# Full-width products as two half-width products side by side in a four-layer graph network on one core

## The chip, the cores and the metric

The kernel runs on one core of a Trainium2 chip. The metric is the device time of one execution in microseconds (us); lower is better. A profiled execution of the kernel is shown beside the times. TensorE is the matrix engine, VectorE and ScalarE are the elementwise engines, GpSimd (POOL) and SyncE (SP) do little here but issue transfers.

## The reference

A dense adjacency matrix `adj` (8192 x 8192, fp32) is multiplied five times by an 8192 x 64 matrix, with a layer norm, a relu, a residual addition and small weight products around each:

```python
h = relu(layernorm(x)); y = h
for k in range(2):                       # layer 0, sweeps 1 and 2
    y = tanh(concat([adj @ y, y]) @ W0[k])
x = x + y
h = relu(layernorm(x)); x = x + adj @ (h @ W1) + bias            # layer 1, sweep 3
h = relu(layernorm(x)); x = x + adj @ (h * (u >= 0.1) / 0.9)     # layer 2, sweep 4
h = relu(layernorm(x))                                           # layer 3, sweep 5
x = x + concat([h, adj @ h / (rowsum(adj) + 1)]) @ W3.T
```

The kernel applies the weights behind the large product, (adj @ h) @ W.

## The kernel before, in words

**Blocks.** The adjacency matrix lies in device memory as 16 x 16 blocks of 512 x 512 numbers, 1 MB each. A block (i, j) takes part in five sweeps, once in each. 775 transfers on SP's queue bring blocks into a ring of 8 slots or into a few held ones, in the order of use; a slot is filled again when TensorE has used the block (and VectorE, if it takes row sums from it).

**Wide and narrow products.** `operand` holds, for each tile of 128 nodes, 128 columns: the 64 features of one sweep and the 64 of the next. Where a block can serve two consecutive sweeps at once, `two_products` (line 632) multiplies it by all 128 columns: four fp32 matmuls with a stationary 128 x 128 operand and a moving 128 x 512 tile. The result has one sweep's features on partitions 0 to 63 and the other's on 64 to 127. Where it serves one sweep, `one_product` (line 604) multiplies it by 64 columns: in each of four steps the first 256 nodes go to partitions 0 to 63 and the other 256 to partitions 64 to 127, with the same stationary 128 x 64 operand. The accumulators are two banks each for wide rows (`double_acc`), narrow rows (`single_acc`), groups taken out of turn (`spare`) and row products (`natural`).

```python
# two_products
acc[:, :], operand[:, b.j * TPB + t, :], stream[:, t, :]
# one_product, h = 0, 1
acc[half_of(h), 0:HALF], operand[:, b.j * TPB + t, half_of(b.row.half)], stream[:, t, nodes_of(h)]
```

**The order of the work.** `make_plan` writes one list, `PLAN`, that all engines follow. Sweeps 1 and 3 run downwards, 2, 4 and 5 upwards, so that the blocks on one side of the diagonal serve two sweeps. A row of 512 nodes has narrow blocks ("single"), wide blocks ("double") and groups out of turn ("late", narrow, and "early", wide). After a row's sum VectorE writes it to `stack` (`take_first`, `take_doubles`); TensorE's `post` multiplies the stacked 128 features by the layer's weights into `natural`; ScalarE or VectorE finishes the row, whose values are an operand of the next sweep. A post is put one block into the next row.

**Own features.** Sweeps 1, 2 and 5 also need the row's own operand, transposed, on the other half of `stack`. ScalarE's `pair_own` copies it, paired, to `own_by_pair` (in sweep 5 four scalings by the degree), TensorE's `turn` transposes it in two full-width transposes into a spare bank, and ScalarE copies it to `stack`. In sweep 1 and 2 the copies are issued a row ahead; in sweep 5 two.

**Posts.** In sweeps 1, 2, 3 and 5 `post` makes eight fp32 products, 64 nodes each as the stationary operand and the 64 weight columns moving, onto alternating halves of the partitions. In sweep 4, whose layer has no weights, it makes two full-width transposes instead, and VectorE writes `stack` in two pieces for them. `degrees` adds the row sums once, by three full-width products.

In the trace each fp32 matmul leaves two MATMUL and two LDWEIGHTS records, a transpose one of each.

Of the kernel before, what the change touches and what calls it, by code (L numbers as in the profile page):

```python
# [36 lines left out]
F = 64  # L37
P = 128
# [387 lines left out]
def gnn_kernel(nc, adj, x, w_both, w_own, bias, u, identity, ones, out):  # L426
# [5 lines left out]
    with ctx:  # L432
# [6 lines left out]
        def sem(name):  # L439
            return ctx.enter_context(nc.semaphore(name))  # L440
# [13 lines left out]
        stack = sb("stack", [P, 2, BLOCK])  # L454
        own_by_pair = sb("own_by_pair", [P, 2, 2, 2 * F])
        deg_part = sb("deg_part", [P, 2 * BLOCK])
# [54 lines left out]
        own_ready = sem("own_ready")  # L511
        own_paired = sem("own_paired")
        tanh_ready = sem("tanh_ready")
# [70 lines left out]
        @block.gpsimd  # L584
        def _(pool):
            pool.memset(w_stack[:, 2, :], 0.0).then_inc(weights_cleared, 1)
            pool.memset(deg_quarter[:, 1:], 0.0).then_inc(deg_cleared, 1)
            for row in ROWS:
                if row.sweep == 3:
                    pool.wait_ge(norm_ready, row.r - 1 - NB)  # L590
                    pool.dma_start(u_in[:, row.r % 2], u[:, tiles(row.i), :]).then_inc(u_loaded[row.r % 2], 16)

        @block.tensor
        def _(pe):
# [37 lines left out]
            def two_products(b, acc):  # L632
                stream = tiles_of(b)
                for t in range(TPB):
                    last = nc.tensor.matmul(  # L635
                        acc[:, :], operand[:, b.j * TPB + t, :], stream[:, t, :],
                        start=b.first and t == 0, stop=b.last and t == TPB - 1)
                return last
# [14 lines left out]
            def turn(row):  # L653

                wait_new(consts_loaded, 16 * CONSTS)
                wait_new(own_paired, rows_with_own(row.r))
                acc = next_spare()
                for k in range(2):
                    last = nc.tensor.transpose(acc[:, k * P:(k + 1) * P], own_by_pair[:, row.r % 2, k, :], ident[:, :])  # L659
                last.then_inc(turned, 1)  # L660

            def post(row):
# [14 lines left out]
                acc = natural[row.r % 2]  # L677
                if row.sweep == 4:
                    to = acc[:, 0:TPB * F].rearrange("p (h k f) -> p k h f", h=2, k=2)
                    for k in range(2):  # L680
                        last = nc.tensor.transpose(to[:, k], stack[:, row.r % 2, k * P:(k + 1) * P],  # L681
                                                   ident[:, :].rearrange("p (h f) -> p h f", h=2))
                else:
                    for t in range(TPB):
                        for c in range(2):
                            nodes = slice(t * P + c * F, t * P + (c + 1) * F)
                            last = nc.tensor.matmul(acc[half_of(c), t * F:(t + 1) * F], stack[:, row.r % 2, nodes],  # L687
                                                    w_stack[:, row.sweep - 1, :], start=True, stop=True)
                last.then_inc(posted, 1)
# [26 lines left out]
        def _(act):  # L716
# [7 lines left out]

            def pair_own(row):

                wait_operand(act.wait_ge, row.sweep, row.i)
                slot = row.r % 2
                if row.sweep == SWEEPS:
                    act.wait_ge(deg_taken, 1)  # L730
                    for t in range(TPB):
                        at = (t % 2) * 2 * F + (t // 2) * F
                        last = nc.scalar.activation(
                            own_by_pair[:, slot].rearrange("p k f -> p (k f)")[:, at:at + F],
                            operand[:, row.i * TPB + t, half_of(row.half)], ACT.Copy, scale=deg_plus[:, row.i, t:t + 1])
                else:
                    own = operand[:, tiles(row.i), half_of(row.half)].rearrange("p (h k) f -> p k h f", k=2)
                    last = nc.scalar.copy(own_by_pair[:, slot].rearrange("p k (h f) -> p k h f", h=2), own)
                last.then_inc(own_paired, 1)

# [7 lines left out]
            act.dma_start(w_stack[upper, 1, :], w_own[lower, 0, :]).then_inc(consts_loaded, 16)  # L748
            act.dma_start(w_stack[lower, 1, :], w_both[lower, 1, :]).then_inc(consts_loaded, 16)
            act.dma_start(w_stack[lower, 4, :], w_own[lower, 1, :]).then_inc(consts_loaded, 16)  # L750
            for to, of in ((bias_sb, bias), (ident, identity)):
                act.dma_start(to[:], of[:]).then_inc(consts_loaded, 16)

            pair_own(ROWS[0])
            for g in range(2, NGROUPS):
                deviation(GROUP, g % 2)
            for what, row in PLAN:
# [8 lines left out]
                elif what == "turn":  # L766
                    if row.r == (SWEEPS - 1) * NB:
                        pair_own(row)
                        pair_own(ROWS[row.r + 1])
                    act.wait_ge(turned, rows_with_own(row.r))  # L770
# [4 lines left out]
                    if row.sweep == SWEEPS and row.i >= 2:  # L775
                        pair_own(ROWS[row.r + 2])
                    elif row.sweep < SWEEPS and row.i != (NB - 1 if row.sweep == 1 else 0):
                        pair_own(ROWS[row.r + 1])
                elif what == "post":
                    if row.sweep <= 2:  # L780
                        act.wait_ge(posted, row.r + 1)
                        got = natural[slot][:, 0:TPB * F].rearrange("p (t f) -> p t f", t=TPB)
                        to = operand[:, tiles(row.i), F:2 * F] if row.sweep == 1 else tanh_out[:, slot]
                        nc.scalar.activation(to, got, ACT.Tanh).then_inc(tanh_ready, 1)  # L784
                        if row.r == NB - 1:
                            pair_own(ROWS[NB])
                    if row.sweep in (2, 3, 4):
# [8 lines left out]
        def _(dve):  # L796
# [83 lines left out]
            def take_first(row):  # L880
# [12 lines left out]
                if not row.single:  # L893
                    if row.sweep == 4:
                        for h in range(2):
                            last = nc.vector.tensor_copy(stack[half_of(h), row.r % 2, 0:HALF], partial[part, row.i, nodes_of(h)])
                    else:
                        last = nc.vector.tensor_copy(stack[part, row.r % 2, :], partial[part, row.i, :])
                else:
# [9 lines left out]
            def take_doubles(row):  # L909
# [6 lines left out]
                else:  # L916
# [5 lines left out]
                    before = partial[part, row.i, :]  # L922
                if row.sweep == 4:
                    for h in range(2):
                        last = nc.vector.tensor_tensor(stack[half_of(h), row.r % 2, 0:HALF], got[part, nodes_of(h)],  # L925
                                                       before[:, nodes_of(h)], ALU.add)
                else:
                    last = nc.vector.tensor_tensor(stack[part, row.r % 2, :], got[part, :], before, ALU.add)  # L928
                last.then_inc(sums_ready, 1)
# [142 lines left out]
```

## Time and profile before

| | before |
|---|---|
| median of 3 runs | 2338.46 us (2338.21 to 2338.47) |
| the profiled execution | 2338.78 us |
| its span | 2337.0 us |
| TensorE busy | 2291.0 us, 98% |
| VectorE busy | 1066.8 us, 46% |
| ScalarE busy | 161.4 us, 7% |
| transfers | 820.78 MB, mean 351 GB/s |

The span is the time between the first and the last record of the profiled execution; what lies between it and the execution's own time (1.8 us) is outside the records. Busy time counts overlapping records once. In the views PE is TensorE's matmul and PEld its weight load, DVE is VectorE, ACT ScalarE; L635 is line 635 of the kernel. A timeline row merges instructions that follow each other and are of one kind; its duration runs to the end of the last record, which overlaps the start of the next row, so that paces are taken from the starts of consecutive rows.

### The profile page before, as it was taken

Reading aid. Unit: us, or ns where it says so; the run is one execution under the profiler, and the core shown is the slowest. Engines: PE = TensorE matmul, PEld = TensorE weight load, DVE = VectorE, ACT = ScalarE, POOL = GpSimd, SP = SyncE. Lnnn points to the kernel's source line nnn. Section 1 sums busy time; section 2 is a strip of 40 time slices with the busy share of each in tenths; the row PEclk is TensorE's granted clock in tenths of the full one; section 3 lists DMA queues with packets and bytes.
Section 4 is the critical chain, followed back from the end, with each engine's and each line's share of the span. In section 5 each row is a group of like instructions: output and inputs, shape, how many; then the busy total and the mean of one; then the engine's idle time right before and its main releaser. Section 6 shows DMA issues by size and latency. Waiting matters only on the chain.

```text
span 2337.0 us, 24750 instructions
## 1 busy us (share of the span) xinstructions
PE 2291.0 (98%) x10118; PEld 1131.9 (48%) x10118; DVE 1066.8 (46%) x2066; ACT 161.4 (7%) x366; POOL 9.5 (0%) x22
## 2 busy tenths in 40 slices
PE   6999999999999999999999999999999999999998
PEld 3454545545454444444444444444455455444465
DVE  7111102114554288887799878887423111101023
ACT  1000000000002210100100000000000000000022
POOL 0000000000000000000000000000000000000000
PEclk9999999999999999999999999999999999999999
DMA  9999999999998878788868888886899999999998
GB/s 388 421 421 421 387 381 378 397 347 377 390 382 293 288 287 303 291 305 300 350 252 356 299 306 310 315 331 256 302 376 389 388 371 389 378 381 376 396 405 363
DMA packets 117904, 820.78 MB, mean 351 GB/s; under 512 B 13856, under 2 KB 18080, under 8 KB 18592
## 3 DMA queue, kind: packets, MB, share of 16 engines
q1 hardware_dynamic: 113904, 814.79, 89.8%
q10 hardware_dynamic: 3120, 2.31, 0.3%
q0 software_dynamic: 768, 2.10, 0.3%
q8 instruction: 80, 1.31, 0.2%
q14 instruction: 32, 0.26, 0.0%
HBM read 817.05 MB, written 2.10 MB: 351 GB/s over the span
## 4 chain that ended last, share of the span: by engine, by line
PE 92%; DMA 5%; DVE 2%; SPq 0%; issue 0%; ACT 0%; DVEq 0%
PE double_acc L635 58%; PE spare L635 12%; PE single_acc L611 11%; PE spare L611 9%; DMA ring<-in_adj 4%; PE natural L687 1%; DMA resid<-in_x 1%; PE spare L659 1%; DVE centred L822 0%; DVE stats L810 0%; DVE partial L878 0%; SPq L574 0%; SPq L581 0%; DVE moments L813 0%; PE natural L681 0%
## 5 line engine op out<-in xcount | busy, mean ns | idle before, releaser
L635 PE MATMUL double_acc<-ring,operand 128*128 128x512 f32 x3136 | 1367.6, 594 | 4.1 <-DVE operand L993 2.6
L635 PEld LDWEIGHTS double_acc<-ring,operand 128*128 128x128 f32 x3136 | 588.9, 190 | 728.2 <-issue 716.5
L611 PE MATMUL single_acc<-ring,operand 128*64 128x256 f32 x2624 | 302.0, 384 | 28.4 <-DVE operand L836 21.8
L635 PE MATMUL spare<-ring,operand 128*128 128x512 f32 x680 | 298.9, 595 | 2.2 <-DMA ring<-in_adj 2.2
L878 DVE TENSOR_TENSOR partial<-spare,partial 64x256 f32<-64x256 f32 (+1 forms) x226 | 105.1, 465 | 421.7 <-PE spare L635 285.2
L859 DVE TENSOR_TENSOR deg_part<-deg_part,ring 128x1024 f32<-128x1024 f32 x213 | 260.9, 1225 | 7.3
L858 DVE TENSOR_TENSOR deg_part<-deg_part,ring 128x1024 f32<-128x1024 f32 x213 | 260.8, 1224 | 6.7
L611 PEld LDWEIGHTS single_acc<-ring,operand 128*64 128x64 f32 x2624 | 183.6, 138 | 150.2 <-DVE operand L836 27.4
L611 PE MATMUL spare<-ring,operand 128*64 128x256 f32 x1840 | 204.7, 380 | 2.1 <-DVE partial L878 2.1
L635 PEld LDWEIGHTS spare<-ring,operand 128*128 128x128 f32 x680 | 126.7, 190 | 157.6 <-issue 154.6
L611 PEld LDWEIGHTS spare<-ring,operand 128*64 128x64 f32 x1840 | 130.8, 137 | 79.5 <-issue 17.5
L925 DVE TENSOR_TENSOR stack<-double_acc,partial 64x256 f32<-64x256 f32 x30 | 12.8, 427 | 319.5 <-PE double_acc L635 319.3
L765 ACT COPY partial<-double_acc 64x512 f32<-64x512 f32 x45 | 26.0, 579 | 1051.7 <-PE double_acc L635 1051.7
L928 DVE TENSOR_TENSOR stack<-double_acc,stack 64x512 f32<-64x512 f32 x26 | 17.7, 682 | 128.6 <-PE double_acc L635 128.5
L822 DVE TENSOR_SCALAR centred<-resid,moments,rsd 128x64 f32<-128x64 f32 x256 | 62.9, 310 | 2.3
L904 DVE TENSOR_TENSOR stack<-single_acc,partial 64x256 f32<-64x256 f32 x80 | 33.6, 420 | 51.4 <-issue 34.9
L784 ACT ACTIVATE operand<-natural 128x256 f32<-128x256 f32 x16 | 6.1, 383 | 643.3 <-PE natural L687 643.3
L687 PEld LDWEIGHTS natural<-w_stack,stack 128*64 128x64 f32 x1024 | 37.9, 138 | 22.8 <-issue 13.2
L928 DVE TENSOR_TENSOR stack<-double_acc,partial 64x512 f32<-64x512 f32 x19 | 13.1, 690 | 73.3 <-PE double_acc L635 73.2
L810 DVE BATCH_NORM_STATS2 stats<-resid 128x6 f32<-128x64 f32 x256 | 38.7, 214 | 12.1 <-DMA resid<-in_x 10.3
L877 DVE COPY partial<-spare 128x512 f32<-128x512 f32 (+1 forms) x19 | 11.5, 607 | 70.3 <-PE spare L635 68.9
L723 ACT ACTIVATE sd<-moments,eps 128x4 f32<-128x4 f32 x64 | 18.9, 297 | 356.0 <-DVE moments L813 356.0
(60 smaller groups left out, 603.5 us busy)
## 6 DMA issues: line engine op xcount, KB each, us to landing
ring<-in_adj SPq DMA_DIRECT2D x756, 1024.0 KB, 7.2
held<-in_adj SPq DMA_DIRECT2D x17, 1024.0 KB, 9.0
resid<-in_x SPq DMA_DIRECT2D x16, 128.0 KB, 16.0
kept<-in_adj SPq DMA_DIRECT2D x2, 1024.0 KB, 11.6
for_layer<-in_u POOLq DMA_DIRECT2D x16, 128.0 KB, 2.4
out_rows<-for_layer ACTq DMA_DIRECT2D x16, 128.0 KB, 7.2
ident<-in_identity ACTq DMA_DIRECT2D x1, 64.0 KB, 10.8
w_stack<-in_w_both ACTq DMA_DIRECT2D x1, 48.0 KB, 8.1
```

The lines of the kernel that those rows point to most:

```text
L611: last = nc.tensor.matmul(acc[half_of(h), 0:HALF], operand[:, b.j * TPB + t, half_of(b.row.half)], stream[:, t, nodes_of(h)], start=b.firs ...
L635: last = nc.tensor.matmul(acc[:, :], operand[:, b.j * TPB + t, :], stream[:, t, :], start=b.first and t == 0, stop=b.last and t == TPB - 1)
L659: last = nc.tensor.transpose(acc[:, k * P:(k + 1) * P], own_by_pair[:, row.r % 2, k, :], ident[:, :])
L687: last = nc.tensor.matmul(acc[half_of(c), t * F:(t + 1) * F], stack[:, row.r % 2, nodes], w_stack[:, row.sweep - 1, :], start=True, stop=True)
L765: nc.scalar.copy(partial[other, row.i, :], double_acc[slot][other, :]).then_inc(partial_saved, 1)
L810: last = nc.vector.bn_stats(stats[:, slot, t, :], values[:, t, :])
L822: last = nc.vector.tensor_scalar(centred[:, t, :], values[:, t, :], moments[:, slot, t, 0:1], rsd[:, t:t + 1], ALU.subtract, ALU.mult)
L858: link(nc.vector.tensor_tensor(acc, acc, data[:, 0:2 * BLOCK], ALU.add))
L859: nc.vector.tensor_tensor(acc, acc, data[:, 2 * BLOCK:], ALU.add).then_inc(deg_added, 1)
L878: return nc.vector.tensor_tensor(to, got, to, ALU.add)
L904: last = nc.vector.tensor_tensor(to, got[half_of(h), 0:HALF], partial[part, row.i, nodes_of(h)], ALU.add)
L928: last = nc.vector.tensor_tensor(stack[part, row.r % 2, :], got[part, :], before, ALU.add)
```

## The change

The wide product becomes two half-width products, one for each sweep's 64 features, each with the whole moving tile of 512 nodes and its own half of the partitions. The turn takes the own operand straight from `operand` (in sweep 5 from a scaled copy) as stationary operand and multiplies it by the identity, on the half of the partitions where it is wanted; the paired copies of sweeps 1 and 2 are gone. The row products of sweep 4 go through the same eight products as the others, with an identity as weights, and VectorE writes `stack` in one piece. The degree sum is as it was.

```diff
-        own_by_pair = sb("own_by_pair", [P, 2, 2, 2 * F])
+        scaled = sb("scaled", [P, 2, TPB, F])
...
-            pool.memset(w_stack[:, 2, :], 0.0).then_inc(weights_cleared, 1)
+            pool.memset(w_stack[:, 2:4, :], 0.0).then_inc(weights_cleared, 1)
...
                 for t in range(TPB):
-                    last = nc.tensor.matmul(
-                        acc[:, :], operand[:, b.j * TPB + t, :], stream[:, t, :],
-                        start=b.first and t == 0, stop=b.last and t == TPB - 1)
+                    for half in range(2):
+                        last = nc.tensor.matmul(
+                            acc[half_of(half), :], operand[:, b.j * TPB + t, half_of(half)], stream[:, t, :],
+                            start=b.first and t == 0, stop=b.last and t == TPB - 1)
...
-                wait_new(own_paired, rows_with_own(row.r))
+                if row.sweep == SWEEPS:
+                    wait_new(own_scaled, row.r + 1 - (SWEEPS - 1) * NB)
+                else:
+                    wait_operand(wait_new, row.sweep, row.i)
                 acc = next_spare()
                 for k in range(2):
-                    last = nc.tensor.transpose(acc[:, k * P:(k + 1) * P], own_by_pair[:, row.r % 2, k, :], ident[:, :])
+                    for h in range(2):
+                        t = 2 * h + k
+                        own = scaled[:, row.r % 2, t, :] if row.sweep == SWEEPS else operand[:, row.i * TPB + t, half_of(row.half)]
+                        last = nc.tensor.matmul(acc[half_of(h), k * P:(k + 1) * P], own, ident[:, :], start=True, stop=True)
...
-                if row.sweep == 4:
-                    to = acc[:, 0:TPB * F].rearrange("p (h k f) -> p k h f", h=2, k=2)
-                    for k in range(2):
-                        last = nc.tensor.transpose(to[:, k], stack[:, row.r % 2, k * P:(k + 1) * P],
-                                                   ident[:, :].rearrange("p (h f) -> p h f", h=2))
-                else:
-                    for t in range(TPB):
-                        for c in range(2):
-                            nodes = slice(t * P + c * F, t * P + (c + 1) * F)
-                            last = nc.tensor.matmul(acc[half_of(c), t * F:(t + 1) * F], stack[:, row.r % 2, nodes],
-                                                    w_stack[:, row.sweep - 1, :], start=True, stop=True)
+                for t in range(TPB):
+                    for c in range(2):
+                        nodes = slice(t * P + c * F, t * P + (c + 1) * F)
+                        last = nc.tensor.matmul(acc[half_of(c), t * F:(t + 1) * F], stack[:, row.r % 2, nodes],
+                                                w_stack[:, row.sweep - 1, :], start=True, stop=True)
...
-                else:
-                    own = operand[:, tiles(row.i), half_of(row.half)].rearrange("p (h k) f -> p k h f", k=2)
-                    last = nc.scalar.copy(own_by_pair[:, slot].rearrange("p k (h f) -> p k h f", h=2), own)
-                last.then_inc(own_paired, 1)
...
-            act.dma_start(w_stack[lower, 1, :], w_both[lower, 1, :]).then_inc(consts_loaded, 16)
+            act.dma_start(w_stack[lower, 1:4:2, :], w_both[lower, 1:4:2, :]).then_inc(consts_loaded, 16)
...
-                if row.sweep == 4:
-                    for h in range(2):
-                        last = nc.vector.tensor_tensor(stack[half_of(h), row.r % 2, 0:HALF], got[part, nodes_of(h)],
-                                                       before[:, nodes_of(h)], ALU.add)
-                else:
-                    last = nc.vector.tensor_tensor(stack[part, row.r % 2, :], got[part, :], before, ALU.add)
+                last = nc.vector.tensor_tensor(stack[part, row.r % 2, :], got[part, :], before, ALU.add)
```

## Rows read from the trace of the kernel before

**Rows 1.** The page: span, TensorE's busy time, its granted clock in 40 slices

```profile
span 2337.0 us, 24750 instructions
PE 2291.0 (98%) x10118; PEld 1131.9 (48%) x10118; DVE 1066.8 (46%) x2066; ACT 161.4 (7%) x366; POOL 9.5 (0%) x22
...
PEclk9999999999999999999999999999999999999999
```

**Rows 2.** Table of stretches: length, busy time by engine, clock, DMA share, GB/s

```profile
157.00:716.00 559.00, 558.92 (x2666) 281.88 (x2666) 155.40 (x203) 19.33 (x51) 0.00 (x0) 1.00 0.97 383
716.00:755.00 39.00, 35.65 (x240) 19.91 (x240) 18.33 (x66) 14.37 (x27) 0.00 (x0) 1.00 0.85 301
755.00:1162.00 407.00, 406.77 (x1135) 182.36 (x1136) 292.44 (x409) 56.90 (x95) 0.67 (x1) 1.00 0.82 303
...
1192.00:1638.00 446.00, 445.90 (x1435) 203.86 (x1433) 369.51 (x535) 11.43 (x27) 6.44 (x12) 1.00 0.82 307
...
1661.00:2225.00 564.00, 563.41 (x2359) 279.62 (x2360) 99.56 (x345) 11.86 (x27) 0.00 (x0) 1.00 0.96 379
2225.00:2337.00 112.00, 102.71 (x1088) 68.01 (x1084) 33.38 (x121) 28.80 (x98) 0.00 (x0) 0.99 0.94 386
```

**Rows 3.** Chain that ended last, in order of time: start, us, what

```profile
142.62 14.24 DMA ring<-in_adj
...
2306.51 18.49 DMA ring<-in_adj
```

**Rows 4.** Groups of instructions, TensorE, shapes apart: the wide products

```profile
L635 PE MATMUL double_acc<-ring,operand 128*128 128x512 f32 x3136 | 1367.6, 594 | 4.1 <-DVE operand L993 2.6 <-DVE operand L988 1.3
...
L635 PE MATMUL spare<-ring,operand 128*128 128x512 f32 x680 | 298.9, 595 | 2.2 <-DMA ring<-in_adj 2.2
...
L635 PE MATMUL double_acc<-held,operand 128*128 128x512 f32 x24 | 10.6, 596 | 0.0
```

**Rows 5.** Timeline of TensorE in sweep 4: start, us, engine, line, tiles, count

```profile
1790.03 12.31 PE L611 MATMUL spare<-ring,operand 128*64 128x256 f32 x112
1802.27 3.70 PE L635 MATMUL double_acc<-ring,operand 128*128 128x512 f32 x8
1805.81 0.38 PE L681 MATMUL natural<-ident,stack 128*128 128x128 f32 x2
1806.03 24.20 PE L635 MATMUL double_acc<-ring,operand 128*128 128x512 f32 x56
1830.15 10.58 PE L611 MATMUL spare<-ring,operand 128*64 128x256 f32 x96
1840.66 3.70 PE L635 MATMUL double_acc<-ring,operand 128*128 128x512 f32 x8
```

**Rows 6.** Timeline of TensorE: a row product among narrow products

```profile
1162.65 1.95 PE L611 MATMUL single_acc<-held,operand 128*64 128x256 f32 x16
1164.43 0.63 PE L687 MATMUL natural<-w_stack,stack 128*64 128x64 f32 x16
1164.90 3.63 PE L611 MATMUL spare<-ring,operand 128*64 128x256 f32 x32
```

**Rows 7.** Timeline of TensorE: the degree sum

```profile
1713.58 1.46 PE L698 MATMUL spare<-deg_quarter,fold_sb 128*128 128x256 f32 x6
1714.87 1.45 PE L635 MATMUL double_acc<-ring,operand 128*128 128x512 f32 x3
```

**Rows 8.** Timeline of TensorE: a turn of sweep 2

```profile
1015.26 0.38 PE L659 MATMUL spare<-ident,own_by_pair 128*128 128x128 f32 x2
1015.48 1.45 PE L635 MATMUL double_acc<-ring,operand 128*128 128x512 f32 x3
```

**Rows 9.** Table of one stretch, line 659 (turns), then line 681 (posts, sweep 4)

```profile
157.00:2225.00 2068.00, 11.90 (x58) 6.94 (x58) 1.00 0.90 345
...
157.00:2225.00 2068.00, 5.84 (x30) 4.06 (x30) 1.00 0.90 345
```

**Rows 10.** Waits of TensorE: us in total, times, longest

```profile
PE single_acc L611 <- DMA ring<-in_adj: 6.2, 10, 0.9
```

More of the change, by code:

```diff
@@ L511, in gnn_kernel @@
         own_ready = sem("own_ready")
-        own_paired = sem("own_paired")
+        own_scaled = sem("own_scaled")
         tanh_ready = sem("tanh_ready")
@@ L723, in deviation, with scale_own @@
                 nc.scalar.activation(sd[:, slot, 0:n], moments[:, slot, 0:n, 1], ACT.Sqrt, bias=eps[:, 0:1]).then_inc(sd_ready, 1)
-            def pair_own(row):
+            def scale_own(row):
                 wait_operand(act.wait_ge, row.sweep, row.i)
[L728 to L735, printed above, removed]
-                else:
-                    own = operand[:, tiles(row.i), half_of(row.half)].rearrange("p (h k) f -> p k h f", k=2)
-                    last = nc.scalar.copy(own_by_pair[:, slot].rearrange("p k (h f) -> p k h f", h=2), own)
-                last.then_inc(own_paired, 1)
+                act.wait_ge(deg_taken, 1)
+                for t in range(TPB):
+                    last = nc.scalar.activation(scaled[:, row.r % 2, t], operand[:, row.i * TPB + t, half_of(row.half)],
+                                                ACT.Copy, scale=deg_plus[:, row.i, t:t + 1])
+                last.then_inc(own_scaled, 1)
             act.wait_ge(eps_set, 1)
@@ L752, in _ @@
                 act.dma_start(to[:], of[:]).then_inc(consts_loaded, 16)
-            pair_own(ROWS[0])
             for g in range(2, NGROUPS):
@@ L767, in _ @@
                     if row.r == (SWEEPS - 1) * NB:
-                        pair_own(row)
-                        pair_own(ROWS[row.r + 1])
+                        scale_own(row)
+                        scale_own(ROWS[row.r + 1])
                     act.wait_ge(turned, rows_with_own(row.r))
@@ L775, in _ @@
                     if row.sweep == SWEEPS and row.i >= 2:
-                        pair_own(ROWS[row.r + 2])
-                    elif row.sweep < SWEEPS and row.i != (NB - 1 if row.sweep == 1 else 0):
-                        pair_own(ROWS[row.r + 1])
+                        scale_own(ROWS[row.r + 2])
                 elif what == "post":
@@ L784, in _ @@
                         nc.scalar.activation(to, got, ACT.Tanh).then_inc(tanh_ready, 1)
-                        if row.r == NB - 1:
-                            pair_own(ROWS[NB])
                     if row.sweep in (2, 3, 4):
@@ L893, in take_first @@
                 if not row.single:
-                    if row.sweep == 4:
-                        for h in range(2):
-                            last = nc.vector.tensor_copy(stack[half_of(h), row.r % 2, 0:HALF], partial[part, row.i, nodes_of(h)])
-                    else:
-                        last = nc.vector.tensor_copy(stack[part, row.r % 2, :], partial[part, row.i, :])
+                    last = nc.vector.tensor_copy(stack[part, row.r % 2, :], partial[part, row.i, :])
                 else:
@@ L922, in take_doubles @@
                     before = partial[part, row.i, :]
-                if row.sweep == 4:
-                    for h in range(2):
-                        last = nc.vector.tensor_tensor(stack[half_of(h), row.r % 2, 0:HALF], got[part, nodes_of(h)],
-                                                       before[:, nodes_of(h)], ALU.add)
-                else:
-                    last = nc.vector.tensor_tensor(stack[part, row.r % 2, :], got[part, :], before, ALU.add)
+                last = nc.vector.tensor_tensor(stack[part, row.r % 2, :], got[part, :], before, ALU.add)
                 last.then_inc(sums_ready, 1)
```

## The prediction

> **What bounds the kernel now.** I read the page first: TensorE is busy for 98% of the span at the full granted clock, the higher of its two levels [rows 1]. No other engine comes near. The table of stretches says where its pace really counts: from 157 us to 2225 us it is never out of work for long, while the last 112 us show gaps [rows 2]. The chain of waits says what bounds the two ends: until 157 us and from about 2225 us it runs through transfers of adjacency blocks [rows 3], and there TensorE only follows. In between stand three short stretches at the turn from one sweep to the next (716 to 755, 1162 to 1192, 1638 to 1661 us), where VectorE's normalisation chain is waited for; the first of them is in [rows 2]. So a shorter stream on TensorE is worth its full length between 157 and 2225 us, about half in the three turns, and nothing at the ends.
>
> The stream is of two kinds. Each fp32 product leaves two records, so a wide block (two sweeps, 128 columns) is 8 records of 512 elements, and a narrow one (one sweep, 64 columns) 16 records of 256 that run two by two. The groups give 3136 and 680 and 24 wide records, thus 480 wide blocks [rows 4]. The mean duration of a record is no pace, since records overlap; the pace comes from starts in the timeline [rows 5]. Two wide runs: 1806.03 to 1830.15 is 24.12 us for 56 records, 1802.27 to 1805.81 is 3.54 us for 8. A step of 0.429 us makes 24.02 and 3.43, which leaves about 0.10 us over in each: in the first because a narrow run follows and starts late, in the second because it comes from a narrow run and its first weight load lies open (it goes over into a full-width transpose without loss). Two narrow runs: 12.24 us for 56 pairs, 10.51 us for 48. The difference, 1.73 us over 8 pairs, is 0.216 us a pair, and each run has 0.15 us over. What a run has too much is a late start of the next (0.09 either way) and an open load at its own start (0.10 wide, 0.05 narrow). A round trip costs 0.10 + 0.10 + 0.15, unrounded **0.347 us**, and these leftovers are what the change removes. That the width does it, not the length of the stream or the accumulator, is in [rows 6]: a narrow block at 1162.65 (after a wide one) is followed by a row product, narrow too but with 64 elements and another bank, after 8 x 0.216 + 0.05 = 1.78 us: the open load alone. The next narrow run starts 0.47 us later.
>
> The Trainium skill (TensorEngine Tiling (Array Packing), Key Properties) says that changing the tiling mode drains the array. The trace agrees, at about 0.09 us each way; the open load comes on top.
>
> **The change, part by part.**
>
> (a) *Wide products as two halves.* 3840 records become 7680 in 3840 pairs. The trace has no pair with 512 elements. Below lies a step of 0.427 us (the 512 elements at the pace of rows, without overhead); above, the nearest row is a pair whose halves do not overlap at all, 2 x 0.429. The value comes from a direct comparison: the degree sum has six undivided records of 256 elements in 1713.58 to 1714.87, 0.215 us each [rows 7], and a pair of half-width ones of the same length has 0.216. Doubling the length doubles the step and adds nothing to it (0.215 against 0.429). I take 0.429 for the pair: cost 0. Its cover: the loads of the next pair run under the present one, as they do now in a narrow pair, which is half as long. If that cover goes, rival 2 has the price.
>
> A second rule speaks against it. The Trainium skill (TensorE: Matmul & The Clock Gate, Part 3) gives a packed group the time of one matmul plus about 4 ns for each further tile; by that rule the sum would lose 15 us and come to 2336.5, where the rows give 2321.5 (an estimate from that page). The narrow pairs here show 1 ns or less.
>
> (b) *Changes of width removed.* TensorE's timeline has 198 of them, 163 between 157 and 2225 us; [rows 5] shows five. Outside the three turns these are 75 round trips (31 to 716 us, 12 to 1162, 18 to 1638, 14 to 2225): 75 x 0.347 = 26.0 us. In 13 of them the first wide work is an own-feature turn, whose load is 0.05 shorter: less 0.6. **Gain 25.4 us.** One round trip is new: the degree sum keeps full width and stood among wide blocks. **Cost 0.35 us.**
>
> (c) *Turns.* Two transposes of one record each take 0.22 us, 1015.26 to 1015.48 [rows 8]. They become four fp32 products, 8 records in 4 pairs, each with 128 elements streaming. A record of that length steps 0.11 us in the same row, so 0.44 us. Ends: 0.06 a pair, the pace of the 64-element pairs of a post (0.47 us over 8 pairs [rows 6]), or 0.22 a pair, that of a pair of 256. 0.11 is the row of the same length. Between 157 and 2225 us there are 58 records [rows 9], 29 turns, 25 outside the three stretches: 25 x 0.22 = **cost 5.5 us**, ends 0 and 16.
>
> (d) *Row products of sweep 4.* Two transposes in 0.22 us (1805.81 to 1806.03 [rows 5]) become the 16 records that every other sweep uses, 0.47 us [rows 6]. Of 15 before 2225 us (30 records [rows 9]) thirteen lie outside the three stretches: 13 x 0.25 = **cost 3.3 us**, ends 0 (the records hidden in the run around them) and 6 (twice the price).
>
> (e) *Other queues.* ScalarE loses the 32 pairing copies of sweeps 1 and 2; the turn then waits for the operand itself, which is ready earlier. The four scalings for sweep 5 stay. VectorE's sums of sweep 4 are one instruction in place of two. Both have slack outside the three stretches; cost 0 there. At the first turn of sweeps a copy less stands ahead of the tanh, some tenths at most. SP and POOL issue what they did; one weight transfer carries one block more, at the very start. The cleared weights reach over one block more.
>
> (f) *The three stretches.* Eight round trips (2.8 us) against 4 turns (0.9) and 2 posts (0.5): 1.4 us shorter, half of it lost to waiting for VectorE: **gain 0.7 us**. At the ends, gain and cost both vanish behind transfers: sweep 5 has 16 of the 48 turns there, 0.22 us more each, but the last stretch follows the transfers, one 1 MB block at a time [rows 3].
>
> Sum: 25.4 - 0.35 - 5.5 - 3.3 + 0.7 = **17.0 us**. The profiled execution took 2338.78 us with a span of 2337.0; it becomes 2321.8. The median of the runs stands 0.3 us under the profiled one: **2321.5 us**. What becomes late next is nothing new; the transfers' share between 157 and 716 us (0.97) and after 1661 (0.96) [rows 2] leaves 3% or more, and 8 us of 559 and 2 us of 564 are asked for.
>
> **Rivals.**
>
> 1. *The gain is held up by transfers or VectorE.* If the stretches with 0.97 and 0.96 [rows 2] are transfer-bound, only 755 to 1638 us gains: 30 round trips, 10.4 us, less 12 turns, 2.6: 7.8 us, **2331**. For it: those shares. Against: TensorE's narrow blocks wait for ring transfers 6.2 us in all, at the ends [rows 10], and VectorE is busy 370 of the 446 us from 1192 on, where it is busiest [rows 2]. Chance 0.10.
>
> 2. *Slower: the weight loads of the two halves are not covered.* Place: each pair in a wide block. The price of an open narrow load is the 0.05 us of [rows 5]. Of the 3840 wide steps 97 come before 157 us, so about 3740 count: +187 us, less the 17 gained, **2508**. It decides from 17.0 / 3740 = 4.5 ns a pair on, a tenth of a load. Against: narrow pairs already load both halves under a stream half as long. Chance 0.07. The Trainium skill (same page, Part 3) says that loads overlap running matmuls only if their row groups differ, and the halves share all rows; the narrow pairs contradict it.
>
> 3. *A few ns more for each pair.* The two halves read the same moving tile a few ns apart; 4 ns by 3740 is 15 us, **2336.5**, no change. Against: 0.216 against 0.215. The rule of the skill weighed in (a) is this case. Chance 0.07.
>
> 4. *The change does not do what it says:* the 0.09 us stay, because they belong to another stream or bank, and only the open loads go. 75 x 0.15 = 11 less 9 is 2 to 3 us, **2336**. [Rows 6] speaks against it. Chance 0.02.
>
> **How the numbers follow.** The forecast has 0.74. About 0.2% (4.7 us) is what a measurement of this kernel can tell from no change. The forecast and rival 1 are faster beyond it, rivals 3 and 4 within it, rival 2 slower; a little is moved from faster to the others, for a pair step off by 3 to 5 ns: 0.82, 0.10, 0.08. The range: below, turns and sweep-4 posts near their low ends give 6 us more, 2315.5; above, turns at their high end cost 10.5 more, 2332, and rival 1 stands at 2331: 2331.5. It leaves out rivals 2 to 4, 0.16.
>
> **What would show it.** In the profile after: a wide block of 16 records in 3.43 us, pair step 0.429; no leftover between wide and narrow runs; 8 records in 0.44 us for a turn and 16 in 0.47 for a sweep-4 post; waits for VectorE at the turns of sweeps longer by about a microsecond; a last stretch of the same length. Wrong it would be if the pair step were 0.433 or more, or if TensorE waited for transfers between 157 and 2225 us.

## The result, and the profile after

| | before | after |
|---|---|---|
| median | 2338.47 us (2338.21 to 2338.72, 4 runs) | 2322.78 us (2322.38 to 2323.25, 4 runs) |
| ratio | | 0.9933, 95% interval 0.9921 to 0.9944 |
| the profiled execution, its span | 2338.78, 2337.0 us | 2323.25, 2321.4 us |

The kernel is 15.7 us (0.67%) faster. Forecast were 2321.5 us and a gain of 17.0, in a range of 2315.5 to 2331.5. A second measurement of the same kernel gave 2322.20 us against 2338.62 before, ratio 0.9931 (0.9917 to 0.9944).

The page of the changed kernel: span and busy time, the costliest groups of the wide products, and VectorE's sums (out<-in xcount | busy, mean ns of one | idle time before).

```profile
span 2321.4 us, 33389 instructions
PE 2273.9 (98%) x14470; PEld 976.4 (42%) x14470; DVE 1064.2 (46%) x2050; ACT 150.3 (6%) x334; POOL 9.6 (0%) x22
...
PEclk9999999999999999999999999999999999999999
...
L636 PE MATMUL double_acc<-ring,operand 128*64 128x512 f32 x6272 | 1362.9, 592 | 4.5 <-DVE operand L973 3.1
...
L636 PE MATMUL spare<-ring,operand 128*64 128x512 f32 x1360 | 297.3, 592 | 2.3 <-DMA ring<-in_adj 2.2
...
L908 DVE TENSOR_TENSOR stack<-double_acc,partial 64x512 f32<-64x512 f32 x34 | 23.5, 692 | 390.9 <-PE double_acc L636 390.8
```

TensorE has 4352 records more than before and is busy 17 us less. The wide groups of [rows 4] have twice the records and nearly the same busy time (1367.6 before, 1362.9 now), as a pair takes the time that one record took. The granted clock is full as in [rows 1], so no part of the difference is a clock.

The part of sweep 4 that answers to [rows 5], in TensorE's timeline after (start, duration, instructions):

```profile
1775.31 12.26 PE L611 MATMUL spare<-ring,operand 128*64 128x256 f32 x112
1787.39 3.60 PE L636 MATMUL double_acc<-ring,operand 128*64 128x512 f32 x16
1790.83 0.63 PE L688 MATMUL natural<-w_stack,stack 128*64 128x64 f32 x16
1791.29 24.20 PE L636 MATMUL double_acc<-ring,operand 128*64 128x512 f32 x112
1815.33 10.53 PE L611 MATMUL spare<-ring,operand 128*64 128x256 f32 x96
1825.69 3.60 PE L636 MATMUL double_acc<-ring,operand 128*64 128x512 f32 x16
```

From start to start, before and after: 56 narrow pairs 12.24 and 12.08 us; a wide block 3.54 and 3.44; the row product 0.22 and 0.46; seven wide blocks 24.12 and 24.04; 48 narrow pairs 10.51 and 10.36. The leftovers of 0.15, 0.10 and 0.08 are gone: 24.04 / 56 is 0.4293 us for a pair, 12.08 / 56 is 0.2157. Over all steady wide steps of the two traces the mean is 0.4292 us both before and after. The row product costs 0.24 more, so that of a round trip of 0.35 some 0.1 is left where sweep 4 has both.

The answer to [rows 8], a turn of sweep 2: 0.43 us from start to start, where it was 0.22.

```profile
1007.38 0.61 PE L666 MATMUL spare<-ident,operand 128*64 128x128 f32 x8
1007.81 3.60 PE L636 MATMUL double_acc<-ring,operand 128*64 128x512 f32 x16
```

The answer to [rows 6], in the timeline after, the row product among narrow ones:

```profile
1154.29 1.90 PE L611 MATMUL single_acc<-held,operand 128*64 128x256 f32 x16
1156.01 0.63 PE L688 MATMUL natural<-w_stack,stack 128*64 128x64 f32 x16
1156.48 3.63 PE L611 MATMUL spare<-ring,operand 128*64 128x256 f32 x32
```

The narrow block that followed a wide one now starts without its open load: 1.72 us to the row product, where it was 1.78. The row product itself keeps its 0.47. And the answer to the first of [rows 3], in the chain that ended last (start, us, what):

```profile
142.28 15.07 DMA ring<-in_adj
```

The transfer that the chain follows up to 157 us ends 0.49 us later than it did before (157.35 against 156.86), so nothing is gained until there.

The gain can be read at any place that both timelines have, by the start of the same block. At the borders of the stretches in [rows 2], each time at the block that starts nearest to the border, it grows like this, beside what the prediction's prices give for each stretch:

```
stretch of before   gain measured   by the prediction's prices
157 to 716 us          7.03         31 x 0.347 - 0.65 - 13 x 0.22        = 7.2
716 to 755             0.12
755 to 1162            1.71         12 x 0.347 - 12 x 0.22               = 1.5
1162 to 1192           0.18
1192 to 1638           5.63         18 x 0.347                           = 6.2
1638 to 1661           0.19
1661 to 2225           1.17         14 x 0.347 - 13 x 0.25 - 0.35        = 1.3
sum                   16.03         (three short stretches together 0.7) = 17.0
```

In the second measurement of the changed kernel the seven numbers are the same to 0.01 us. What differs between these two executions lies outside: the first 157 us and the last 110.

### The profile page after: what moved, and what is told of

Read it like the earlier page. It is cut to its first block, busy times and chain, and to the rows that moved or that the text cites. A ratio compares the mean times of both kernels' runs of the same rounds, so it can differ in the third digit from the quotient of the medians.

```text
span 2321.4 us, 33389 instructions
## 1 busy us (share of the span) xinstructions
PE 2273.9 (98%) x14470; PEld 976.4 (42%) x14470; DVE 1064.2 (46%) x2050; ACT 150.3 (6%) x334; POOL 9.6 (0%) x22
## 4 chain that ended last, share of the span: by engine, by line
PE 91%; DMA 6%; DVE 2%; issue 0%; SPq 0%; ACT 0%; DVEq 0%
PE double_acc L636 58%; PE spare L636 12%; PE single_acc L611 10%; PE spare L611 9%; DMA ring<-in_adj 5%; PE natural L688 1%; DMA resid<-in_x 1%; PE spare L666 1%; DVE centred L811 0%; DVE partial L867 0%; DVE stats L799 0%; DVE moments L802 0%; SPq L574 0%; SPq L581 0%; ACT sd L724 0%
## 5 line engine op out<-in xcount | busy, mean ns | idle before, releaser
L636 PE MATMUL double_acc<-ring,operand 128*64 128x512 f32 x6272 | 1362.9, 592 | 4.5 <-DVE operand L973 3.1
L636 PEld LDWEIGHTS double_acc<-ring,operand 128*64 128x64 f32 x6272 | 445.4, 137 | 860.1 <-issue 846.4
L636 PE MATMUL spare<-ring,operand 128*64 128x512 f32 x1360 | 297.3, 592 | 2.3 <-DMA ring<-in_adj 2.2
L908 DVE TENSOR_TENSOR stack<-double_acc,partial 64x512 f32<-64x512 f32 x34 | 23.5, 692 | 390.9 <-PE double_acc L636 390.8
L636 PEld LDWEIGHTS spare<-ring,operand 128*64 128x64 f32 x1360 | 97.0, 137 | 182.8 <-issue 177.3
L611 PEld LDWEIGHTS spare<-ring,operand 128*64 128x64 f32 x1840 | 132.7, 137 | 75.4 <-issue 13.5
L688 PEld LDWEIGHTS natural<-w_stack,stack 128*64 128x64 f32 x1280 | 49.5, 138 | 29.6 <-issue 16.5
L688 PE MATMUL natural<-w_stack,stack 128*64 128x64 f32 x1280 | 50.1, 222 | 4.0 <-DVE stack L908 1.9
L866 DVE COPY partial<-spare 128x512 f32<-128x512 f32 (+1 forms) x19 | 11.5, 607 | 70.6 <-PE spare L636 69.2
```

What stands on the lines that cost most here:

```text
L611: last = nc.tensor.matmul(acc[half_of(h), 0:HALF], operand[:, b.j * TPB + t, half_of(b.row.half)], stream[:, t, nodes_of(h)], start=b.firs ...
L636: last = nc.tensor.matmul(acc[half_of(half), :], operand[:, b.j * TPB + t, half_of(half)], stream[:, t, :], start=b.first and t == 0, stop ...
```

## The experiments

**One part alone: the wide products.** The kernel before with this edit only:

```diff
                 for t in range(TPB):
-                    last = nc.tensor.matmul(
-                        acc[:, :], operand[:, b.j * TPB + t, :], stream[:, t, :],
+                    for half in range(2):
+                        last = nc.tensor.matmul(
+                            acc[half_of(half), :], operand[:, b.j * TPB + t, half_of(half)], stream[:, t, :],
```

> The kernel before with the wide products as two halves, and nothing else: turns and the row products of sweep 4 stay full-width transposes. Theory (every change of width costs a drain of 0.09 us and an open load): between 157 and 2225 us 163 changes of width become 90, all around the 29 turns, 15 posts of sweep 4 and the degree sum, at 0.093 + 0.056 + 0.094 + 0.05 = 0.293 us a round trip. Against the changed kernel that is 44 x 0.293 = 12.9 us more, less 29 x 0.22 + 15 x 0.25 = 10.1 for the cheaper transposes: +2.5 to 2.8, about 2325.4 us. Rival A (the gain comes from ScalarE and VectorE, which have less to do): no gain here, 2338. Rival B (the identity products in half width are a loss that should have been left out): this kernel beats the changed one, 2312 to 2315.

Measured: 2325.18 us, ratio 0.9941 (0.9926 to 0.9956). That is 2.4 us above the changed kernel, as the theory has it. The two were not measured side by side; the kernel before took 2339.15 us beside this one and 2338.47 beside the other. The traces need no such comparison: between the block that starts at 157 us and the one at 2225 us this kernel gains 13.2 us on the kernel before, where the changed kernel gains 16.0. The timeline of this kernel shows both kinds of transposes standing alone in full width, first a turn, then a row product of sweep 4:

```profile
1009.09 0.44 PE L660 MATMUL spare<-ident,own_by_pair 128*128 128x128 f32 x2
1009.45 3.65 PE L636 MATMUL double_acc<-ring,operand 128*64 128x512 f32 x16
...
1792.80 0.44 PE L682 MATMUL natural<-ident,stack 128*128 128x128 f32 x2
1793.17 24.25 PE L636 MATMUL double_acc<-ring,operand 128*64 128x512 f32 x112
```

A transposing turn or row product now takes 0.36 to 0.37 us (0.22, its load open for 0.05, the late start behind it 0.09), and with the late start ahead and the open load after, the round trip has eaten what the transposes save. Rival A is out: ScalarE and VectorE work as they did before, and all but 2 to 3 us of the gain is there. Rival B is out too: the identity products pay, by a little.

**The other part alone.** The changed kernel with `two_products` as it was before, so that only turns and row products are in half width.

> The changed kernel with the wide products undivided again: only turns and the row products of sweep 4 are half-width. Theory: 211 changes of width between 157 and 2225 us against 163 before, 24 round trips more at 0.347 us = 8.3, 29 turns x 0.22 = 6.4 and 15 posts x 0.25 = 3.8: 18.5 us more than before, less about 1.5 hidden between the sweeps: slower, about 2356 us. Rival A (less work for ScalarE and VectorE brings the gain): at or under 2338. Sum check: the two parts alone give about -13 and +17, together -15.7, so the parts must not add up.

Measured: 2357.64 us, ratio 1.0080 (1.0065 to 1.0095), slower by some 18.5 us where about 17 was expected. The turn and the wide block behind it in this kernel:

```profile
1025.33 0.66 PE L665 MATMUL spare<-ident,operand 128*64 128x128 f32 x8
1025.92 3.70 PE L635 MATMUL double_acc<-ring,operand 128*128 128x512 f32 x8
1029.55 0.69 PE L687 MATMUL natural<-w_stack,stack 128*64 128x64 f32 x16
```

The turn is 0.59 us (0.44 and 0.15 of an open load and a late start), the wide block 3.63 (3.43 and 0.20). The two parts are worth about 14.0 and -18.5 us alone (both against 2339.15 us, the kernel before measured beside them) and 15.7 together: the identity products in half width pay only where the products around them are in half width too.

**More round trips, and nothing else changed.** In the changed kernel every second wide block of the rows of sweeps 2 and 3 is undivided again:

```diff
+                if b.row.sweep in (2, 3) and b.j % 2:
+                    for t in range(TPB):
+                        last = nc.tensor.matmul(
+                            acc[:, :], operand[:, b.j * TPB + t, :], stream[:, t, :],
+                            start=b.first and t == 0, stop=b.last and t == TPB - 1)
+                    return last
                 for t in range(TPB):
                     for half in range(2):
```

> The changed kernel, but in the rows of sweeps 2 and 3 every wide block with an odd column is an undivided product, every other one two halves. Both kinds have the same length of stream (512) and the same bank. Theory (the width alone makes the cost): 240 changes of width are added between 157 and 2225 us, 120 round trips x 0.347 = 41.6 us: about 2364 us, each full-width block starting 0.10 us late on the way in and 0.09 on the way out. Rival C (the 0.09 us belong to a change of bank or of the length of the stream, the width only opens loads): 120 x 0.15 = 18, about 2341 us.

Measured: 2364.41 us, ratio 1.0111 (1.0096 to 1.0126), 41.6 us above the changed kernel's 2322.78, for 120 round trips: 0.347 us each, the price taken from the kernel before. Here too the kernel before took 2339.15 us beside the one and 2338.47 beside the other, so that 0.7 us of it may belong to the two measurements; between the same two blocks near 157 and 2225 us the traces differ by 40.8 us, 0.340 each.

```profile
999.37 3.70 PE L636 MATMUL double_acc<-ring,operand 128*128 128x512 f32 x8
1003.00 3.65 PE L642 MATMUL double_acc<-ring,operand 128*64 128x512 f32 x16
1006.58 3.70 PE L636 MATMUL double_acc<-ring,operand 128*128 128x512 f32 x8
```

Both kinds of block write the same bank and stream 512 elements. The full-width one takes 3.63 us to the next start, the divided one 3.58, together 7.21 where two blocks without a change are 6.87. So rival C (18 us) falls, and with it the prediction's rival 4: the change of width makes the cost, without a change of bank or of streamed length.

**The start.** The changed kernel with undivided wide products in its first 60 blocks (the same edit with `b.number < 60` as the condition). It brings back 12 changes of width before 157 us, and a seventh round trip there and back at 157 and 164 us.

> The changed kernel with undivided wide products in the first 60 blocks alone, up to about 160 us, where TensorE follows the transfers. Theory (the ends are bound by transfers): 12 changes of width are back there, 6 round trips or 2.1 us of TensorE's time, and the time stays that of the changed kernel, 2322.8 within 0.5 us. Rival D (each round trip counts wherever it lies): 2.1 to 2.4 us more, 2325 us.

Measured: 2324.38 us, ratio 0.9939 (0.9923 to 0.9956), 1.6 us above the changed kernel's first measurement, which fits neither theory. The changed kernel and this one were therefore measured again side by side.

> The changed kernel once more, beside the two below on one chip, as the measure for differences of 0.5 to 2 us: 2322.8 us, or what 15.7 us less than the kernel before is on this chip.

> The kernel with undivided wide products in the first 60 blocks again; its first measurement stood 1.6 us above the changed kernel's and 0.7 us of that may be the chip. Theory (the ends are bound by transfers): within 0.5 us of the changed kernel run beside it. Rival D (each round trip counts wherever it lies): 2.1 us above it. If it comes out near 1 us, a part of the stretch before 160 us is TensorE's own.

Measured: 2322.20 us for the changed kernel and 2323.42 for the other, ratios 0.9931 (0.9917 to 0.9944) and 0.9936 (0.9923 to 0.9948). The difference is 1.2 us, again more than the 0.5 us of the theory and less than the 2.1 of rival D. The traces show where it lies. TensorE's timeline of the changed kernel (second measurement):

```profile
157.14 3.65 PE L636 MATMUL spare<-ring,operand 128*64 128x512 f32 x16 [0.54 <-DMA ring<-in_adj]
160.62 7.04 PE L636 MATMUL double_acc<-ring,operand 128*64 128x512 f32 x32
167.49 1.90 PE L611 MATMUL spare<-held,operand 128*64 128x256 f32 x16
...
2216.82 12.69 PE L611 MATMUL spare<-ring,operand 128*64 128x256 f32 x116
...
2316.52 0.69 PE L688 MATMUL natural<-w_stack,stack 128*64 128x64 f32 x16 [0.55 <-DVE stack L889]
```

and of the kernel with the undivided start:

```profile
156.95 3.70 PE L636 MATMUL spare<-ring,operand 128*128 128x512 f32 x8 [0.20 <-DMA ring<-in_adj]
160.48 3.60 PE L636 MATMUL double_acc<-ring,operand 128*128 128x512 f32 x8
164.01 3.65 PE L642 MATMUL double_acc<-ring,operand 128*64 128x512 f32 x16
167.49 1.90 PE L611 MATMUL spare<-held,operand 128*64 128x256 f32 x16
...
2216.82 12.69 PE L611 MATMUL spare<-ring,operand 128*64 128x256 f32 x116
...
2314.53 1.95 PE L611 MATMUL single_acc<-ring,operand 128*64 128x256 f32 x16 [0.62 <-DMA ring<-in_adj]
2316.31 0.64 PE L694 MATMUL natural<-w_stack,stack 128*64 128x64 f32 x16
2317.49 0.69 PE L694 MATMUL natural<-w_stack,stack 128*64 128x64 f32 x16 [0.55 <-DVE stack L895]
```

Both start the same block at 167.49 us, the one after waiting 0.54 us for a transfer at its last stop, the other after 0.20. The six round trips before that stop have vanished in the wait. The seventh, behind the stop, costs 0.19 us (10.54 against 10.35 us to the block at 167.49); in this pair a transfer that landed 0.19 us earlier hides it, in the first pair of traces 0.10 us of it is left (167.84 against 167.74 us). From 167.49 up to 2216.82 us the kernels agree to 0.01 us. So rival D, in which the round trips themselves cost their 2.1 us, falls.

The rest of the difference, 0.97 us between the last rows, arises in the last 40 us, where the two run the same instructions: the last transfer, issued 0.10 us later, lands 1.29 us later, and one more block is waited for. In the first pair of traces, too, about 1.0 us arises in the waits for transfers there. From the last wide block to the last row product it takes 107.9 to 108.7 us in the five kept traces whose first 60 blocks are divided, and 108.9 and 109.7 in the two with the undivided start. Either kernel has nine times in the two measurements. Those with the undivided start are all 2323.17 us or more; of the changed kernel's only two are. That it came out so in both measurements speaks against mere scatter. Why the last transfers end later with the undivided start stays open: the theory's "within 0.5 us" missed both times, and what is shown is only that the first end hides the round trips themselves.

**The last round trip.** The changed kernel with the degree sum in half width too:

```diff
-                    last = nc.tensor.matmul(acc[:, 0:NB * SQUARES], fold_sb[:, :],
-                                            deg_quarter[:, part].rearrange("p i b -> p (i b)"), start=part == 0, stop=part == PARTS - 1)
+                    for half in range(2):
+                        last = nc.tensor.matmul(acc[half_of(half), 0:NB * SQUARES], fold_sb[:, half_of(half)],
+                                                deg_quarter[:, part].rearrange("p i b -> p (i b)"), start=part == 0, stop=part == PARTS - 1)
```

> The changed kernel with the degree sum in half width too, three products as six, so that no change of width is left at all. Theory: one round trip less, 0.35 us (0.09 late into the sum and its load open for 0.10, 0.09 late out of it and the next load open for 0.05), and the six records become six pairs of the same 0.215 us: about 2322.4 us, which the times alone can hardly tell from 2322.8; the trace is to show the wide run before, the sum and the run after without a leftover. Rival F (the sum waits for VectorE or a bank there anyway): no gain in the trace either.

> The version with no change of width left, again: 0.35 us under the changed kernel run beside it, if the times can show it at all; not above it.

Measured: 2322.25 us, ratio 0.9930 (0.9915 to 0.9945), and the second time 2322.07 us, 0.9929 (0.9917 to 0.9942), 0.1 under the changed kernel beside it. It is the fastest version of this study, by less than the times can tell. The degree sum in TensorE's timeline of the changed kernel:

```profile
1698.90 1.56 PE L699 MATMUL spare<-deg_quarter,fold_sb 128*128 128x256 f32 x6
1700.40 5.80 PE L636 MATMUL double_acc<-ring,operand 128*64 128x512 f32 x26
```

And in that of this version:

```profile
1698.37 1.47 PE L700 MATMUL spare<-deg_quarter,fold_sb 128*64 128x256 f32 x12
1699.66 5.75 PE L636 MATMUL double_acc<-ring,operand 128*64 128x512 f32 x26
```

1.50 us become 1.29, the same as in [rows 7]; 0.21 of the 0.35 us lie here, the rest in the wide runs ahead of it and behind; over the whole stretch between 157 and 2225 us the trace gains 0.39 us on that of the changed kernel. Rival F is out in the trace.

**The order of the halves.** The changed kernel, with the four products of one half ahead of the four of the other in the wide rows of sweep 2:

```diff
+                if b.row.sweep == 2:
+                    for half in range(2):
+                        for t in range(TPB):
+                            last = nc.tensor.matmul(
+                                acc[half_of(half), :], operand[:, b.j * TPB + t, half_of(half)], stream[:, t, :],
+                                start=b.first and t == 0, stop=b.last and t == TPB - 1)
+                    return last
```

> The changed kernel, but in the wide rows of sweep 2 (120 blocks) all four products of one half come first, then all four of the other. Products, operands and widths are the same; only the neighbours in the stream are no longer on different columns. Theory (a pair costs one step because its two neighbours run at once; TensorE starts matmuls in program order): a block of 16 records takes 14 to 16 steps of 0.429 us where it took 8, so 120 x 6 x 0.429 = 309 to 120 x 8 x 0.429 = 412 us more: 2632 to 2735 us. Rival E (the engine finds the overlap whatever the order): 2323 us.

Measured: 2375.25 us, ratio 1.0156 (1.0139 to 1.0173): 52 us more than the changed kernel, not 309 to 412, and not nothing. Both theories as I had put them are wrong. TensorE's timeline at a row product of sweep 2 shows why:

```profile
801.55 0.33 PE L695 MATMUL natural<-w_stack,stack 128*64 128x64 f32 x2
801.98 1.02 PE L637 MATMUL double_acc<-ring,operand 128*64 128x512 f32 x2
802.41 0.33 PE L695 MATMUL natural<-w_stack,stack 128*64 128x64 f32 x2
802.84 0.59 PE L637 MATMUL double_acc<-ring,operand 128*64 128x512 f32 x1
803.26 0.45 PE L695 MATMUL natural<-w_stack,stack 128*64 128x64 f32 x9
803.55 0.59 PE L637 MATMUL double_acc<-ring,operand 128*64 128x512 f32 x1
```

The row product stands behind the whole wide block in the program, yet its first records start at 801.55, 1.3 us ahead of the block's last at 802.84. So a record can start ahead of others that wait for columns still busy, if its own columns are free. At the beginning of a row four records start alone, 0.43 us apart, and only with the fifth does the other half begin. The weight loads behind this row product show it, first one at a step and then more:

```profile
803.99 0.14 PEld L637 LDWEIGHTS double_acc<-ring,operand 128*64 128x64 f32 x1 [0.23 <-issue]
804.41 0.14 PEld L637 LDWEIGHTS double_acc<-ring,operand 128*64 128x64 f32 x1 [0.29 <-issue]
804.84 0.14 PEld L637 LDWEIGHTS double_acc<-ring,operand 128*64 128x64 f32 x1 [0.29 <-issue]
805.27 0.19 PEld L637 LDWEIGHTS double_acc<-ring,operand 128*64 128x64 f32 x3 [0.29 <-issue]
```

The other half had gone past three records of the first that stood before it, and so had the row product at 801.55. In steady state 16 records take 3.55 us (8 starts in 1.773, again and again), nearly the 3.43 of pairs. That is about 0.11 us a block, 13 us over 120 blocks; the other 39 lie at the ends of the rows.

To see whether a shorter distance is free, the same with two products of one half, then two of the other:

```diff
+                if b.row.sweep == 2:
+                    for t in range(0, TPB, 2):
+                        for half in range(2):
+                            for s in range(t, t + 2):
+                                last = nc.tensor.matmul(
+                                    acc[half_of(half), :], operand[:, b.j * TPB + s, half_of(half)], stream[:, s, :],
+                                    start=b.first and s == 0, stop=b.last and s == TPB - 1)
+                    return last
```

> The changed kernel, but in the wide rows of sweep 2 two products of one half, then two of the other, and the same again. With all four of a half together the block took 3.55 us in steady state, not the 6 to 7 us of strict order, so the engine let the other half overtake. Theory now: it can start a matmul ahead of some three others that wait for their columns, so a distance of four records costs nothing within a row: the block takes 3.43 to 3.50 us, with a fill and an emptying of one or two steps at each row's ends, 15 rows x 1 us or less: 2323 to 2340 us. If the engine kept program order: 4 records alone for each 8, 120 blocks x 2 to 4 steps x 0.429: 2426 to 2530 us.

Measured: 2322.46 us, ratio 0.9930 (0.9917 to 0.9944), no different from the 2322.20 us of the changed kernel on the same chip. Its rows in the timeline:

```profile
984.52 22.54 PE L638 MATMUL double_acc<-ring,operand 128*64 128x512 f32 x104
1006.84 0.66 PE L674 MATMUL spare<-ident,operand 128*64 128x128 f32 x8
```

104 records in 22.32 us are 0.4292 us for two, the step of the changed kernel. At a distance of four records the order costs nothing, at eight it does.

## Why the prediction was right

- **The bound.** TensorE's stream between 157 and 2225 us set the time, the ends did not. Both traces of the changed kernel gain 16.0 us between those marks, where their spans are 15.6 and 16.6 us shorter in all. The undivided start showed that the first end hides round trips. That such a start costs nothing in all did not hold: that kernel was 1.2 us slower, by waits for transfers in the last stretch, and why is open. Waits of TensorE for transfers outside the ends did not appear, so rival 1 did not come: the transfers' share after, 0.98 between 148 and 709.7 us, was still not the limit.
- **(a) The pair.** Forecast 0.429 us, the pace of an undivided record; measured 0.4293 in the rows shown and 0.4292 over the whole stream, as before. Neither the 4 ns of the Trainium skill's packed groups (TensorE: Matmul & The Clock Gate, Part 3) nor an open load appears, and rivals 2 and 3 are settled: 3740 steps at 4 ns would have been 15 us.
- **(b) The change of width.** Forecast 0.347 us a round trip; the run with 120 of them more gave 0.340 by the traces and 0.347 by the times. The drain named by the Trainium skill (TensorEngine Tiling (Array Packing), Key Properties) agrees with the late starts in these traces, about 0.09 us each way, and a little over half of the round trip's price comes from them; the rest is the open load. (The prediction says that [rows 5] shows five changes of width; it shows three, and nothing is worked out from the number.)
- **(c), (d) Turns and row products.** Forecast 0.44 and 0.47 us, measured 0.43 and 0.46 to 0.47. The choice of the row with the same number of elements was right for both.
- **(e) Other queues.** ScalarE and VectorE are busy 11 and 3 us less, which did nothing for the end: the kernel with the wide products alone, in which they work as before, has all but the 2 to 3 us that its extra round trips cost. "Cost 0" outside the three stretches was not quite right: just behind the second of them, at 1193.74 us of the trace after (1202.69 us before), a wide block waits 0.24 us for an operand that VectorE writes, and 0.20 us of the gain already made is lost again there.
- **(f) The short stretches.** Forecast 0.7 us, measured 0.5. TensorE's waits for VectorE between 157 and 2225 us grew from 10.9 to 11.5 us in all, less than the microsecond at each turn that was named as a sign.
- **What was off.** 17.0 us were forecast where 16.0 arose between the marks and 15.5 in the profiled execution. Of the first 1.0 us, half is a count in (b): between the marks of the table the four long stretches hold 61, 25, 34 and 27 changes of width, 73.5 round trips where 75 were priced. With these counts the prices give 7.1, 1.7, 5.9 and 1.1 us, beside 7.03, 1.71, 5.63 and 1.17 measured. What is then left is the wait for VectorE at 1193.74 us (0.2) and the short stretches (0.2). The other 0.5 us lies in the ends: the profiled execution entered the stretch at 157 us 0.5 us late; in the second measurement it was 0.2 late there and gained 0.8 in the last stretch. So the stretches that follow transfers differ by 0.2 and 0.8 us between these two executions of one kernel.

## What to carry to other kernels

Where a stream on TensorE mixes products of 128 and of 64 columns, take the price of a change of width from consecutive starts in the timeline, count the changes that lie where TensorE is the bound, and weigh them against what the uniform width costs; here splitting the wide ones cost nothing. Begin with the wide ones: alone they brought 14.0 of the 15.7 us. The small products converted alone made the kernel 18.5 us slower; they pay only once the products around them are in half width. Price each converted piece by the row with the same streamed length, and count on nothing from the stretches that follow transfers.

## What the runs showed of the hardware that was not expected

- **Matmuls on different columns overtake each other.** A row product's records started 1.3 us ahead of a wide record that the program has first. With halves four records apart nothing was lost (2322.46 against 2322.20 us on the same chip), with halves eight apart 52 us over 120 blocks. The Trainium skill (TensorE: Matmul & The Clock Gate, Part 3, The mechanism) has matmuls strictly in order in start and end; by the starts in these traces this does not hold between column halves.
- **Two halves that read the same moving tile cost what one full-width product costs**, 0.4292 us in either kernel for 512 elements.
- **The last 110 us, which follow transfers, differ by up to 0.8 us** between two executions of the changed kernel whose gains over the 2068 us before agree to 0.01 us.
